# Loads of the expert stage issued one 128-row tile at a time, instead of two tiles in one DMA

## The chip, the core and the metric

The kernel runs on one NeuronCore of a Trainium2 chip. The metric is the device time of one execution in microseconds (us); lower is better. The engines are named as in the profile: PE (TensorE, matmul) with its weight loads PEld, DVE (VectorE), ACT (ScalarE), POOL (GpSimd) and SP (SyncE), which computes nothing and issues DMAs.

## What is computed

16 batches of 512 tokens with 256 features pass a layer norm, a linear attention and a feed-forward part with 16 routed experts (4 for each token) and a shared one:

```python
xn = _layernorm(x, axis=-1)
x = x + attn(xn) + ffn(xn)
# ffn, T = 8192 tokens, H = 256, E = 16 experts, I = 128
combine = _route(x, gate_weight)                 # (T, E), 4 weights of a token are not zero
up = jnp.einsum('th,ehi->eti', x, expert_up)
down = jnp.einsum('eti,eih->eth', jax.nn.silu(up), expert_down)
moe_out = jnp.einsum('te,eth->th', combine, down)
shared = jax.nn.silu(x @ shared_up) @ shared_down
```

The kernel computes an expert only for the tokens that are routed to it.

## The kernel before

**First stage** (to about 469 us of the profiled span). For each batch the kernel normalises, computes the attention, the shared expert and the routing. POOL scatters each token's row of features and weights into `by_expert`, a table in DRAM with a region for each expert. A row of it has two halves of `RW` = 272 floats: the token's features with its routing weights, and the running sum of its outputs.

**Expert stage** (the rest). The work is cut into `UNITS` = 143 units. A unit is one expert and `UR` = 256 rows of the table, held in SBUF as two tiles of 128 rows. A unit `u` passes these steps:

- SP: `load_rows(u)` brings the unit's first halves into `f_rows[u % 8]` (names `x_in` and `xn` in the trace, line 424). It waits until PE has done `up` of unit `u - 6` (semaphore `fu_done`), which frees the buffer. `load_sums(u)` brings the second halves into `f_y[u % 8]` (`xn`, line 434), after waits on `added[k]`, the landings of earlier units' scatters (line 433). The first row's number is in a register, read from a table in SBUF; `four_from` (line 323) reads the numbers of four units in one TENSOR_LOAD, for the row numbers and for each of the four classes of `added`.
- PE: `turn_rows(u)` (line 1446) waits for `rows_loaded[u % 8]` and transposes the rows into PSUM, 4 matmuls a unit; `up` (line 316, into `bank_x`) and `down` (line 316, into `bank_a` or `bank_y`) follow.
- ACT: rounds the transposed rows (698), the silu (719), rounds its result (724), stages the weights (708).
- DVE: copies the unit's weights out of the rows (1242, waits for `rows_loaded`), the low parts (1245, 1268), then `sum_up(u)` (1251 and 1257, waits for `acc_loaded[u % 8]`), which adds the outputs to the sums.
- POOL: scatters the sums back with two indirect DMAs (574).

On each engine the order is written out by hand. SP's is `load_rows(0)`, `load_rows(1)`, ..., with sums three units behind rows:

```python
            ROWS_AHEAD = 7
            SUMS_AHEAD = 4
            for u in range(UNITS + ROWS_AHEAD):
                if u < UNITS:
                    load_rows(u)
                if 0 <= u - (ROWS_AHEAD - SUMS_AHEAD) < UNITS:
                    load_sums(u - (ROWS_AHEAD - SUMS_AHEAD))
```

After the last unit SP stores the sums to the output in eight DMAs (451).

Of the kernel before, what the change touches and what calls it, by code (L numbers as in the profile page):

```python
# [12 lines left out]
P = 128  # L13
# [8 lines left out]
def attention_and_routed_ffn(  # L22
# [33 lines left out]
    YB = 8  # L56
# [23 lines left out]
    with ExitStack() as ctx:  # L80
# [3 lines left out]
        def sem(name):  # L84
            return ctx.enter_context(nc.semaphore(name))
# [4 lines left out]
        def wait(eng, s, value):  # L90
            if value > 0:
                eng.wait_ge(s, value)

        def reused(t, shape, at=0, partitions=P):
            names = " ".join("abcd"[:len(t.shape) - 1])
            flat = t[tuple(slice(None) for _ in t.shape)].rearrange(f"p {names} -> p ({names})")
            size = 1
            for n in shape:
                size *= n
            names = " ".join("abcd"[:len(shape)])  # L100
            return flat[0:partitions, at:at + size].rearrange(f"p ({names}) -> p {names}",
                                                              **dict(zip("abcd", shape)))
# [150 lines left out]
        RB = 8  # L253
        f_y = [reused(xn, (2, RW), (i + 4) % 8 * 2 * RW) for i in range(YB)]
        f_rows = [reused(xn, (2, RW), (YB + i) * 2 * RW) for i in range(4)]
# [37 lines left out]
        rows_loaded = [sem(f"rows_loaded{i}") for i in range(RB)]  # L293
        fx_done, fx_hi, fx_lo, fw_ready, w2_ready = sems("fx_done", "fx_hi", "fx_lo", "fw_ready", "w2_ready")
        fu_done, fs_done, fh_hi, fh_lo, fd_done = sems("fu_done", "fs_done", "fh_hi", "fh_lo", "fd_done")
        acc_loaded = [sem(f"acc_loaded{i}") for i in range(YB)]
# [8 lines left out]
        def scatters_until(c):  # L305
            return BATCH_SCATTERS * (c // NB + 1)

        def adds_until(u):
            return PRIMED + 32 * (u // CLS + 1)
# [11 lines left out]
        def four_from(engine, i, u, low, high):  # L321
            if u % 4 == 0:
                fours[engine, i] = fours.get((engine, i), ())[-4:] + nc.values_load_multi_w_load_instructions(
                    table[i:i + 1, u // P, u % P:u % P + 4], engines=[engine], min_val=low, max_val=high,
                    skip_runtime_bounds_check_because="the plan makes every entry, and makes it within these bounds")[1]
            return fours[engine, i][-4 + u % 4]
# [6 lines left out]
        def expert_from(words, u):  # L333
            return (words[u // PACK] >> 4 * (u % PACK)) & (E - 1)
# [16 lines left out]
        def _(sp):  # L351
# [34 lines left out]

            def unit_rows(first_row, half):
                return by_expert[bass.ds(first_row, UR), half * RW:(half + 1) * RW].rearrange(
                    "(s p) r -> p s r", p=P)

            zero_rows = [SPARE] + [FIRST + e * REGION for e in range(E)] + [OVER + i * OVER_ROWS for i in range(OVERS)]

# [22 lines left out]
            row_of = {}  # L415

            def load_rows(u):
                wait(sp, fu_done, u - RB + 3)
                row_of[u] = four_from(mybir.EngineType.SP, 0, u, 0, SLOTS - UR)
                if u < EARLY:  # L420
                    sp.wait_ge(scattered[(B - 1) % NB], four_from(mybir.EngineType.SP, 2 + CLS, u, scatters_until(B - 1 - NB),
                                                                  scatters_until(B - 1)))
                    sp.sem_inc(rows_whole, 1)
                sp.dma_start(f_rows[u % RB], unit_rows(row_of[u], 0)).then_inc(rows_loaded[u % RB], 16)

            def load_sums(u):
                if u == 4:
                    sp.wait_ge(scattered[(B - 1) % NB], scatters_until(B - 1))
                if u >= YB:
                    sp.wait_ge(added[(u - YB) % CLS], adds_until(u - YB))  # L430
                for k in range(CLS):
                    sp.wait_ge(added[k], four_from(mybir.EngineType.SP, 2 + k, u, PRIMED, PRIMED + 32 * UNITS))
                    sp.sem_inc(sums_free, 1)
                sp.dma_start(f_y[u % YB], unit_rows(row_of.pop(u), 1)).then_inc(acc_loaded[u % YB], 16)

            ROWS_AHEAD = 7
            SUMS_AHEAD = 4
# [5 lines that stand above are left out]
# [286 lines left out]
        def _(dve):  # L729
# [507 lines left out]

            def rows_low(u):
                expert = expert_from(experts, u)
                dve.wait_ge(rows_loaded[u % RB], 16 * (u // RB + 1))  # L1240
                wait(dve, y_ready, u - 3)
                V.tensor_copy(w2[:, u % 4, :], f_rows[u % RB][:, :, bass.ds(expert + D, 1)]  # L1242
                              .rearrange("p s o -> p (s o)")).then_inc(w2_ready, 1)
                dve.wait_ge(fx_hi, u + 1)
                V.tensor_tensor(f_l[u % 4], A[u % 2][:, :].rearrange("p (c s t) -> p c s t", c=KD, s=2),  # L1245
                                f_h[u % 4].bitcast(F32), ALU.subtract).then_inc(fx_lo, 1)

            def sum_up(u):
                expert = expert_from(experts, u)
                dve.wait_ge(acc_loaded[u % YB], 16 * (u // YB + 1))  # L1250
                V.tensor_tensor(f_id[:, u % YB, :], f_y[u % YB][:, :, bass.ds(expert + D, 1)].bitcast(U32)
                                .rearrange("p s o -> p (s o)"), nowhere[:, u % YB, :], ALU.max).then_inc(id_ready, 1)
                dve.wait_ge(fd_done, u + 1)
                dve.wait_ge(w2_ready, u + 1)
                for tile in range(2):
                    y = f_y[u % YB][:, tile, 0:D]
                    last = V.scalar_tensor_tensor(out=y, in0=f_dn[u % 2][tile][:, 0:D], scalar=w2[:, u % 4, tile:tile + 1],  # L1257
                                                  in1=y, op0=ALU.mult, op1=ALU.add)
                last.then_inc(y_ready, 1)

            rows_low(0)
            rows_low(1)
            for u in range(UNITS + 1):
                if u + 2 < UNITS:
                    rows_low(u + 2)
                if u < UNITS:
                    dve.wait_ge(fh_hi, u + 1)
                    V.tensor_tensor(f_hl[u % 2], f_hid[u % 2], f_hh[u % 2].bitcast(F32), ALU.subtract  # L1268
                                    ).then_inc(fh_lo, 1)
                if u >= 1:  # L1270
                    sum_up(u - 1)

        @block.tensor
        def _(pe):
# [164 lines left out]
            last.then_inc(plan_turned, 1)  # L1439

            def turn_rows(u):
                pe.wait_ge(rows_loaded[u % RB], 16 * (u // RB + 1))
                wait(pe, fx_lo, u - 1)
                for h in range(KD):
                    for tile in range(2):
                        last = T_.transpose(A[u % 2][:, (2 * h + tile) * P:(2 * h + tile + 1) * P],  # L1446
                                            f_rows[u % RB][:, tile, h * P:(h + 1) * P], ident[:, :])
                last.then_inc(fx_done, 1)

            pe.wait_ge(plan_ready, 1)  # L1450
            experts = load_experts(mybir.EngineType.PE)
            turn_rows(0)
            turn_rows(1)
            for u in range(UNITS + 1):
                if u < UNITS:
# [50 lines left out]
```

## Time and profile before

| | before |
|---|---|
| median of 3 runs | 972.61 us (971.91 to 973.69) |
| time of the profiled execution | 966.78 us |
| its span, first to last instruction | 964.8 us |
| PE, DVE, ACT, POOL busy, of the span | 80%, 73%, 57%, 60% |
| first rows loaded, last scatter issued | 469.2 us, 947.7 us |

The profiled execution is 5.8 us below the median of the runs and 2.0 us above its own span. The granted TensorE clock was 0.929 of full speed over the span. Busy shares leave out SP: its instructions wait, move registers or issue DMAs, and the profile shows when they start and how long they take.

### The profile page before, as it was taken

What the parts mean: (1) busy time and instruction counts of PE and PEld (TensorE: products, weight loads), DVE (VectorE), ACT (ScalarE), POOL (GpSimd) and SP (SyncE); (2) the same over time, 40 slices, a digit from 0 to 9 for tenths busy, and PEclk for the clock granted to TensorE, in tenths of its full rate; (3) what the DMA queues carried; (4) which work ended last, traced back from release to release, by engine and by line L of the source; (5) the groups of instructions that cost most, each with busy time, mean ns of one, the idle gap of its engine ahead of it and who ended that gap; (6) DMA issues with size and microseconds to landing.
All of it is one profiled execution on the core that took longest, in us unless ns stands there. A gap on an engine that the chain in (4) does not pass through costs nothing. (4 is left out here: it accounts for less than half of the span.)

```text
span 964.8 us, 19765 instructions
## 1 busy us (share of the span) xinstructions
PE 768.8 (80%) x5264; PEld 704.2 (73%) x5264; DVE 700.7 (73%) x2390; ACT 553.1 (57%) x1142; POOL 581.4 (60%) x581
## 2 busy tenths in 40 slices
PE   4999999999999999997377767687676776776760
PEld 4899999999899988886266666676675775765750
DVE  5989898888888999999466555665556665656550
ACT  5677677676677766663155545554545544555440
POOL 1067766666777766666556565665555566656662
PEclk9999999999999999999599899998889888999795
DMA  5245554554445433332599888888887887888889
GB/s 156 71 171 193 186 176 179 194 187 175 149 159 188 146 129 129 114 116 112 177 288 284 239 266 266 252 261 268 245 252 250 270 267 247 265 264 261 249 277 304
DMA packets 142316, 202.15 MB, mean 210 GB/s; under 512 B 16176, under 2 KB 117184, under 8 KB 142208
## 3 DMA queue, kind: packets, MB, share of 16 engines
q1 hardware_dynamic: 114144, 116.47, 41.8%
q0 software_dynamic: 28064, 84.43, 22.8%
q8 instruction: 45, 0.74, 0.3%
q14 instruction: 63, 0.52, 0.2%
HBM read 104.19 MB, written 105.04 MB: 217 GB/s over the span
## 5 line engine op out<-in xcount | busy, mean ns | idle before, releaser
L574 POOL DMA_INDIRECT rows_by_expert<-xn,f_id x286 | 279.8, 978 | 194.4 <-issue 64.5
L490 POOL DMA_INDIRECT rows_by_expert<-xn,slots_now x192 | 196.9, 1026 | 122.8 <-PE bank_a L316 59.1
L1245 DVE TENSOR_TENSOR xt_l<-bank_a,xt_h 128x512 fp32r<-128x512 f32 x143 | 98.3, 687 | 97.1 <-ACT xt_h L698 67.4
L719 ACT ACTIVATE hid<-bank_x 128x256 f32<-128x256 f32 x143 | 55.3, 387 | 147.3 <-PE bank_x L316 71.5
L698 ACT CAST xt_h<-bank_a 128x512 fp32r<-128x512 f32 x143 | 83.8, 586 | 77.7 <-PE bank_a L1446 49.7
L316 PE MATMUL bank_y<-we,hs_h 128*128 x284 | 68.0, 333 | 68.4 <-DVE hs_l L1268 45.3
L316 PE MATMUL bank_a<-we,hs_h 128*128 x288 | 70.0, 337 | 61.9 <-DVE hs_l L1268 42.5
L316 PEld LDWEIGHTS bank_y<-we,hs_h 128*128 128x128 f32 x284 | 49.4, 210 | 82.3 <-issue 82.2
L316 PEld LDWEIGHTS bank_a<-we,hs_h 128*128 128x128 f32 x288 | 51.4, 216 | 75.0 <-issue 74.6
L316 PE MATMUL bank_y<-ws,hs_h 128*128 128x256 f32 x512 | 94.4, 282 | 1.4 <-DVE hs_l L997 1.4
L316 PE MATMUL bank_x<-xt_h,ws 128*128 128x512 f32 x256 | 92.1, 401 | 0.0
L496 POOL DMA_INDIRECT rows_by_expert<-xn,slots_now x64 | 80.0, 1250 | 17.9 <-issue 14.2
L316 PEld LDWEIGHTS bank_y<-ws,hs_h 128*128 128x128 f32 x512 | 80.9, 188 | 4.4 <-DVE hs_l L997 1.6
L1257 DVE SCALAR_TENSOR_TENSOR xn<-bank_a,w,xn 128x256 f32<-128x256 f32 x144 | 62.6, 476 | 15.1 <-PE bank_y L316 10.9
L316 PE MATMUL bank_y<-ws,hs_l 128*128 128x256 f32 x256 | 72.3, 282 | 0.0
L1257 DVE SCALAR_TENSOR_TENSOR xn<-bank_y,w,xn 128x256 f32<-128x256 f32 x142 | 61.8, 476 | 13.3 <-PE bank_a L316 10.2
L316 PE MATMUL bank_x<-xt_h,k_h 128*128 128x256 f32 x288 | 70.8, 306 | 0.0
L316 PE MATMUL bank_x<-xt_h,k_l_p 128*128 128x256 f32 x284 | 68.1, 301 | 0.0
L651 ACT ACTIVATE k_f<-bank_a,minus_one 128x256 f32<-128x256 f32 x64 | 30.4, 475 | 57.5 <-issue 41.4
L1268 DVE TENSOR_TENSOR hs_l<-hid,hs_h 128x256 fp32r<-128x256 f32 x143 | 60.0, 420 | 2.8 <-ACT hs_h L724 2.8
L724 ACT CAST hs_h<-hid 128x256 fp32r<-128x256 f32 x143 | 59.5, 416 | 0.1
L1446 PE MATMUL bank_a<-ident,xn 128*128 128x128 f32 x288 | 48.6, 296 | 12.6 <-DMA xn<-rows_by_expert 12.6
(289 smaller groups left out, 2427.7 us busy)
## 6 DMA issues: line engine op xcount, KB each, us to landing
xn<-rows_by_expert SPq DMA_DIRECT2D x215, 272.0 KB
x_in<-rows_by_expert SPq DMA_DIRECT2D x71, 272.0 KB
rows_by_expert<-spare SPq DMA_DIRECT2D x22, 544.0 KB
x_in<-in_L_attn_x_dram SPq DMA_DIRECT2D x16, 512.0 KB
out_dram<-rows_by_expert SPq DMA_DIRECT2D x8, 1024.0 KB
rows_by_expert<-xn,f_id POOLq DMA_INDIRECT x286
rows_by_expert<-xn,slots_now POOLq DMA_INDIRECT x256
w_raw<-in_L_ffn_expert_up_dram SPq DMA_DIRECT2D x32, 64.0 KB
```

Of the source, the lines that this page charges most:

```text
L316: last = nc.tensor.matmul(dst, a, b, start=start and k == 0, stop=stop and k == n - 1, skip_group_check=mixed)
L490: G.indirect_dma_start(out=half_rows[:, :], in_=xn[:, c % NB, s, 0:RW], in_offset=None, out_offset=bass.IndirectOffsetOnAxis(ap=slots_now[ ...
L496: G.indirect_dma_start(out=by_expert[:, :], in_=xn[:, c % NB, s, :], in_offset=None, out_offset=bass.IndirectOffsetOnAxis(ap=slots_now[:, ...
L574: G.indirect_dma_start(out=half_rows[:, :], in_=f_y[u % YB][:, tile], in_offset=None, out_offset=bass.IndirectOffsetOnAxis(ap=f_id[:, u % ...
L651: S_.activation(k_f[:, s, :], A[s][:, 0:D], ACT.Exp, bias=minus_one[:, 0:1])
L698: S_.copy(f_h[u % 4], A[u % 2][:, :].rearrange("p (c s t) -> p c s t", c=KD, s=2)).then_inc(fx_hi, 1)
L719: S_.activation(f_hid[u % 2], X[u % 2][:, 0:UR], ACT.Silu).then_inc(fs_done, 1)
L724: S_.copy(f_hh[u % 2], f_hid[u % 2]).then_inc(fh_hi, 1)
L1245: V.tensor_tensor(f_l[u % 4], A[u % 2][:, :].rearrange("p (c s t) -> p c s t", c=KD, s=2), f_h[u % 4].bitcast(F32), ALU.subtract).then_inc ...
L1257: last = V.scalar_tensor_tensor(out=y, in0=f_dn[u % 2][tile][:, 0:D], scalar=w2[:, u % 4, tile:tile + 1], in1=y, op0=ALU.mult, op1=ALU.add)
L1268: V.tensor_tensor(f_hl[u % 2], f_hid[u % 2], f_hh[u % 2].bitcast(F32), ALU.subtract).then_inc(fh_lo, 1)
L1446: last = T_.transpose(A[u % 2][:, (2 * h + tile) * P:(2 * h + tile + 1) * P], f_rows[u % RB][:, tile, h * P:(h + 1) * P], ident[:, :])
```

## The change

`unit_rows` now yields the tiles one by one, and `load_rows` and `load_sums` issue one DMA for each tile of 128 rows. Both DMAs of a unit count on the semaphore of the buffer, so what was a wait for 16 (times the turn of the buffer) is now a wait for 32. Nobody starts on one tile alone. Bytes, buffers, and the order of units are as they were.

```diff
             def unit_rows(first_row, half):
                 return by_expert[bass.ds(first_row, UR), half * RW:(half + 1) * RW].rearrange(
-                    "(s p) r -> p s r", p=P)
+                    "(s p) r -> s p r", p=P)
...
-                sp.dma_start(f_rows[u % RB], unit_rows(row_of[u], 0)).then_inc(rows_loaded[u % RB], 16)
+                for tile in range(2):
+                    sp.dma_start(f_rows[u % RB][:, tile], unit_rows(row_of[u], 0)[tile]).then_inc(rows_loaded[u % RB], 16)
...
-                sp.dma_start(f_y[u % YB], unit_rows(row_of.pop(u), 1)).then_inc(acc_loaded[u % YB], 16)
+                first_row = row_of.pop(u)
+                for tile in range(2):
+                    sp.dma_start(f_y[u % YB][:, tile], unit_rows(first_row, 1)[tile]).then_inc(acc_loaded[u % YB], 16)
...
             def rows_low(u):
                 expert = expert_from(experts, u)
-                dve.wait_ge(rows_loaded[u % RB], 16 * (u // RB + 1))
+                dve.wait_ge(rows_loaded[u % RB], 32 * (u // RB + 1))
...
             def sum_up(u):
                 expert = expert_from(experts, u)
-                dve.wait_ge(acc_loaded[u % YB], 16 * (u // YB + 1))
+                dve.wait_ge(acc_loaded[u % YB], 32 * (u // YB + 1))
...
             def turn_rows(u):
-                pe.wait_ge(rows_loaded[u % RB], 16 * (u // RB + 1))
+                pe.wait_ge(rows_loaded[u % RB], 32 * (u // RB + 1))
```

SP's program, early in the expert stage, before. An ISA row computes the address of the DMA behind it in registers; waits are named where they stand ahead of a row:

```order
L323 TENSOR_LOAD q_f [waits fu_done]
L424 ISA
L424 DMA xn<-rows_by_expert 128x2x272
L434 ISA [waits added0,added1,added2,added3]
L434 DMA xn<-rows_by_expert 128x2x272
L424 ISA [waits fu_done]
L424 DMA xn<-rows_by_expert 128x2x272
```

The same kind of place now (lines 424 and 434 have become 425 and 437):

```order
L323 TENSOR_LOAD q_f [waits fu_done]
L425 ISA
L425 DMA x_in<-rows_by_expert 128x272
L425 ISA
L425 DMA x_in<-rows_by_expert 128x272
L437 ISA [waits added1,added0,added2,added3]
L437 DMA xn<-rows_by_expert 128x272
L437 ISA
L437 DMA xn<-rows_by_expert 128x272
L425 ISA [waits fu_done]
```

Each load has become two pairs of ISA and DMA, and no wait stands between the two. In the whole of SP's program that is 286 pairs more, two for each of 143 units; the table reads and the waits stand where they stood. The other engines have the same instructions in the same order.

## Rows read from the trace of the kernel before

**Rows 1.** Windows view, all engines, steady part of the expert stage (busy us, instructions).
```profile
core 0: us, PE busy (x) PEld busy (x) DVE busy (x) ACT busy (x) POOL busy (x), PEclk, DMA share, GB/s
500.00:920.00 420.00, 301.31 (x2056) 277.09 (x2054) 259.75 (x772) 220.06 (x517) 251.91 (x258) 0.90 0.84 259
```

**Rows 2.** Waits view, PE, 500 to 920 us: in total, times, longest.
```profile
PE bank_y L316 <- DVE hs_l L1268: 42.5, 21, 4.4
PE bank_a L316 <- DVE hs_l L1268: 37.5, 19, 4.2
...
```

**Rows 3.** Windows view of line 1446 alone (PE's transposes, 4 matmuls a unit).
```profile
core 0: us, PE busy (x) PEld busy (x), PEclk, DMA share, GB/s
480.00:500.00 20.00, 5.62 (x32) 4.05 (x31) 0.91 0.88 273
...
500.00:920.00 420.00, 85.30 (x516) 66.15 (x516) 0.90 0.84 259
```

**Rows 4.** View of line 1446: what ended PE's idle time before it (us, times).
```profile
  DMA xn<-rows_by_expert: 26.3, 6
```

**Rows 5.** Waits view, SP's queue, 500 to 920 us: all of it.
```profile
SPq L433 <- DMA rows_by_expert<-xn,f_id: 31.2, 31, 3.4
SPq L424 <- remote: 7.2, 6, 1.6
SPq L424 <- PE bank_x L316: 7.0, 8, 1.5
SPq L323 <- PE bank_x L316: 2.1, 3, 1.0
SPq L323 <- remote: 0.4, 1, 0.4
```

**Rows 6.** Timeline of SP's queue (start us, us of one issue).
```profile
484.40 0.37 SPq L424 DMA_DIRECT2D x_in<-rows_by_expert  x1
485.25 0.37 SPq L434 DMA_DIRECT2D xn<-rows_by_expert  x1
...
502.08 0.37 SPq L434 DMA_DIRECT2D xn<-rows_by_expert  x1
502.64 0.37 SPq L424 DMA_DIRECT2D x_in<-rows_by_expert  x1
...
504.62 0.70 SPq L424 DMA_DIRECT2D x_in<-rows_by_expert  x1
505.66 0.37 SPq L434 DMA_DIRECT2D xn<-rows_by_expert  x1
506.62 0.37 SPq L424 DMA_DIRECT2D x_in<-rows_by_expert  x1
```

**Rows 7.** Views of lines 424, 433, 323: ns min/median/max, first and last start.
```profile
L424 SPq FUSED_REGOPS  x131: 3/37/699, 500.3 to 919.4; - x131
L424 SPq MOVE x_in<-rows_by_expert x66: 2/29/709, 501.0 to 917.9; - x66
...
L433 SPq EVENT_SEMAPHORE  x572: 3/17/4505, 478.3 to 929.1; - x191
...
L323 SPq TENSOR_LOAD <-q_f x161: 3/298/1400, 499.6 to 913.9; - x161
```

**Rows 8.** DMA view, 500 to 920 us: queue, packets, MB, share of 16 engines.
```profile
q1 hardware_dynamic: 70515, 72.22, 61.8%
```

**Rows 9.** DMA view, 500 to 920 us: issues of the loads.
```profile
xn<-rows_by_expert SPq DMA_DIRECT2D x194, 272.0 KB
x_in<-rows_by_expert SPq DMA_DIRECT2D x66, 272.0 KB
```

## The prediction, made before the changed kernel ran

> **What bounds the kernel now.** The change touches only the expert stage, so I read that stage. First the windows view of its steady part [rows 1]: in 420 us PE is busy 301 us (72%), DVE 62%, ACT 52%, POOL 60%, and the DMA engines 84% at 259 GB/s. No engine is full. Then who is waited for: PE's longest waits end with DVE's low part of the hidden rows [rows 2], the chain PE, ACT, DVE, PE of one unit. No wait of PE in this stretch ends with a load; the waits that do, 26.3 us in 6 times [rows 4], lie at the start. So loads are early, and the pace is one unit in 3.26 us: 516 transposes, 4 a unit, are 129 units in 420 us [rows 3].
>
> Last the queue that the change makes longer, SP's. The reader should see two things in it. It waits little: its waits add up to 47.9 us [rows 5], 0.37 us a unit. And it is not idle in the rest. Two gates hold SP back: rows wait for `up` of an older unit, sums for landings of old scatters. A queue with time to spare would stand at one of them in every unit. The waits view names 49 such stops [rows 5], for the 260 loads [rows 9]. So in most units SP stands at no gate and runs as fast as it can, in 3.26 - 0.37 = 2.89 us a unit.
>
> **What the change adds on SP.** Each load gets a second pair of address computation and DMA. The nearest row is exact: where SP goes from a sums load to the next rows load with no stop, the two DMAs start 0.56 us apart (502.08 to 502.64) [rows 6], and between them stand just the first DMA's issue (0.37 us), one register operation and one move (medians 37 and 29 ns [rows 7]), the rest being gaps. The added pair is this sequence, so 0.56 us, and 1.12 us a unit with two loads.
>
> **What SP's unit costs.** From rows to sums without a stop, four semaphore instructions included, it is 0.85 us (484.40 to 485.25) [rows 6]; back to rows 0.56. That is 1.41. Table reads: 161 for 129 units, median 298 ns [rows 7], 0.37 us a unit. Together 1.78 us, if nothing disturbs it. The difference to the 2.89 us above, 1.11 us, is time that the waits view doesn't name: the same rows show it as steps of 1.04 and 0.96 us where 0.85 and 0.56 would do (from 504.62 on) [rows 6], and as maxima of 699 ns and more for instructions of 30 ns [rows 7]. It is either a slowness of SP under load, which stays, or waits that the view missed, which an SP that is later would not have to make.
>
> - If all of it is missed waits: 1.78 + 1.12 = 2.90 us a unit, under 3.26. SP fits.
> - If all of it stays: 2.89 + 1.12 = 4.01 us. SP sets the pace, 0.75 us a unit slower.
>
> I take two thirds of the 1.11 us as staying (0.74), nearer to the upper end, because the delays also fall on the register instructions, which wait for nothing: 1.78 + 0.74 + 1.12 = 3.64 us a unit. SP then becomes the bound; PE, DVE, ACT and POOL, which have room at 3.26, wait for loads. (3.64 - 3.26) x 143 units = 54 us.
>
> **The start of the stage.** From 480 to 500 us PE turns 8 units in 20 us, 2.5 us each [rows 3], and this is where it already waits for loads. Counting all 143 units at 3.26 leaves out that these 8 went faster: at the new pace they lose 8 x (3.26 - 2.5) = 6 us more.
>
> **What costs nothing.** Bytes stay. Each new DMA ends with its counts on 16 engines: taking them as whole packets, 32 more a unit, 2 on each engine. A packet of the hardware queue takes 0.618 x 16 x 420 us / 70,515 = 59 ns [rows 8], so at most 0.12 us a unit, of 0.52 us that the engines are free (16% of 3.26); below this they cost nothing. The second tile's data starts 0.56 us later than now; consumers wait for both tiles, but no PE wait ends with a load in the steady part [rows 2], so as long as SP keeps its lead this is hidden, and if the lead is gone it is in SP's sum already. Nothing else is queued on SP but the waits on `added` and the table reads, and they stand behind the longer issue; who waits for them is again the loads. The drain after the last unit, POOL's last scatters and the stores, is as before. The wait for 32 instead of 16 is free.
>
> **Whether an issue is small.** A unit's load is 272 KB [rows 9], 278.5 thousand bytes, 1.08 us at 259 GB/s; a half is 0.54 us, so an added pair of 0.56 us is as long as the transfer it starts. The Trainium skill, page DMA: Bandwidth & Descriptors, section Issuing engines are not separate DMA queues, says that the sequencer's time to start a DMA is usually small relative to the DMA itself. By that rule the added time would be 0 and the kernel the same. For a half load the trace disagrees.
>
> **The sum.** 54 + 6 = 60 us on the profiled execution's 966.8 us: 1026.8. The median of the runs is 5.8 us above it, so 1033 us.
>
> **Rivals.**
>
> - *SP just fits.* All of the 1.11 us are missed waits; 2.90 us a unit is under 3.26. For it: the delays come in lumps, and may be of the record rather than of the queue. Against it: SP's few stops. The steady pace stays, but in the start SP's 2.90 meets PE's 2.5: 8 x 0.4 = 3 us; 976 us, slower by 0.35%. Chance 0.15.
> - *No change.* The same, and the loads in the start are hidden too, since SP's own waits there for scatters cover the added issues: 973 us. This is also what the skill's rule gives. Chance 0.10.
> - *Everything stays.* 4.01 us a unit: 0.75 x 143 + 6 = 113 us, 1086 us. It is the upper end of the forecast's own term. If the new instructions are slowed as the old ones are, by 2.89 / 1.78, the 1.12 becomes 1.82 us, 4.71 us a unit, and the time 966.8 + 1.45 x 143 + 6 + 5.8 = 1186 us. Chance 0.05 for beyond 1088.
> - *Faster.* One mechanism: a DMA of one tile reads 128 rows in the order in which they lie, and half as much stands in a queue at once, so POOL's scatters get their turn on the 16 engines sooner. SP's 31.2 us of waits on their landings [rows 5] would shrink; at most all go, 942 us. It decides only if SP has more than 1.12 us a unit to spare and if landings set the pace, and PE's waits [rows 2] name none. Chance 0.05.
> - *Forecast*: SP sets the pace, between 3.3 and 4.0 us a unit. Chance 0.65.
>
> **How the numbers follow.** The time is the forecast's, 1033. What a measurement can tell from no change is about 0.2%, 2 us. The range goes from the rival that just fits, 976, to the end where everything stays, 1088; it leaves out no change, faster, and the multiplied cost, 0.20 together. Slower is forecast, just fits and multiplied, 0.85; same 0.10; faster 0.05.
>
> **What the changed profile would show.** Right: two issues of a load 0.5 to 0.6 us apart; SP's named waits near zero, since it never reaches a gate; waits of PE's transposes or DVE's weight copy on DMA landings all through the stage, not in the start alone; a unit in about 3.6 us; DMA share down from 0.84 to about 0.75; PE's busy time nearly the same, with perhaps a lower granted clock as it idles more. Wrong: SP's named waits still a few tenths of a microsecond a unit and no wait of PE on a load, which would say that SP had time to spare. The weakest step is the split of the 1.11 us.

## The result, and the profile after

The changed kernel takes 1039.64 us (median of 4 runs, 1035.4 to 1041.53), the kernel before on the same chip 973.15 us (4 runs, 971.91 to 975.35). The ratio is 1.0675, 95% interval 1.0636 to 1.0713: slower. The profiled execution took 1041.53 us, with a span of 1039.4 us, 74.6 us more than before, at a granted clock of 0.912. Lines have moved: rows are loaded at 425, sums at 437, the wait for older scatters is 434, PE's transposes are 1449, DVE's weight copy 1245.

Read in the order in which the prediction read the kernel before. First the windows of the steady part, all engines:

```profile
core 0: us, PE busy (x) PEld busy (x) DVE busy (x) ACT busy (x) POOL busy (x), PEclk, DMA share, GB/s
520.00:980.00 460.00, 303.81 (x1993) 276.53 (x1992) 260.76 (x746) 218.13 (x498) 238.40 (x248) 0.88 0.76 227
```

and of the transposes alone (columns as in [rows 3]):

```profile
480.00:500.00 20.00, 5.36 (x26) 3.85 (x27) 0.79 0.65 189
520.00:980.00 460.00, 92.53 (x496) 60.94 (x496) 0.88 0.76 227
```

496 transposes are 124 units in 460 us, **3.71 us a unit**, where [rows 3] gave 3.26 and the prediction 3.64. Every engine is less busy than in [rows 1] (PE 66% of the stretch, was 72%), and so are the DMA engines, 0.76 at 227 GB/s after 0.84 at 259. So none of these became the bound. The 8 fast units at the start are gone too: 26 transposes are 6.5 units in the same 20 us, 3.1 us each, where there were 8 at 2.5.

Who is waited for has turned round. Waits view of SP's queue, 520 to 980 us, all of it:

```profile
SPq L323 <- DMA rows_by_expert<-xn,f_id: 3.4, 12, 0.4
SPq L434 <- DMA rows_by_expert<-xn,f_id: 1.6, 3, 0.7
```

Waits view of PE, the same stretch, its longest rows:

```profile
PE bank_a L1449 <- DMA x_in<-rows_by_expert: 70.4, 44, 3.6
PE bank_a L1449 <- DMA xn<-rows_by_expert: 69.1, 43, 3.6
```

and of DVE:

```profile
DVE w L1245 <- DMA x_in<-rows_by_expert: 19.8, 22, 2.8
DVE w L1245 <- DMA xn<-rows_by_expert: 16.4, 17, 1.7
```

SP stands at a gate for 5.0 us in all, against 47.9 us before [rows 5], though the stretch is longer. PE waited on no load in the steady part before; now it waits 139.5 us on loads, 87 times in 124 units. In [rows 2] the low part of the hidden rows was what PE waited for; it is no longer among the long ones. SP's queue, its issues from 700 us on (start, time of the row, number of issues in it):

```profile
699.97 0.85 SPq L425 DMA_DIRECT2D x_in<-rows_by_expert  x2
701.39 0.87 SPq L437 DMA_DIRECT2D xn<-rows_by_expert  x2
702.44 0.85 SPq L425 DMA_DIRECT2D x_in<-rows_by_expert  x2
705.86 0.85 SPq L437 DMA_DIRECT2D xn<-rows_by_expert  x2
```

and the instructions of the rows' line (ns min/median/max):

```profile
L425 SPq FUSED_REGOPS  x248: 2/37/1398, 521.5 to 979.2; - x124
L425 SPq DMA_DIRECT2D x_in<-rows_by_expert x125: 3/333/1397, 519.8 to 969.6; - x125
L425 SPq MOVE x_in<-rows_by_expert x124: 4/29/719, 521.6 to 969.5; - x124
L425 SPq MOVE xn<-rows_by_expert x124: 2/29/726, 530.3 to 979.3; - x124
```

Two issues take 0.85 us together and one 0.333 us, so they start 0.52 us apart. An issue of 128 rows takes 333 ns, of 2 x 128 rows 0.37 us [rows 6]. Where nothing is in the way, rows to sums is 1.42 us (699.97 to 701.39) and back 1.05 (701.39 to 702.44); before, 0.85 and 0.56. Then 3.42 us pass between rows and sums (702.44 to 705.86), with no wait named. The trace has in them four table reads of 0.30 us each, which stand there in every fourth unit, and a step of 0.72 us just ahead of the first issue; that issue, of 333 ns elsewhere, is recorded with 22 ns. The page has the chain of work that ended last, and the loads' DMA queue:

```profile
SPq 16%; issue 15%; DMA 11%; PE 6%; POOL 2%; DVE 2%; ACT 1%; POOLq 0%; another core or an unknown queue 0%; DVEq 0%; ACTq 0%
...
q1 hardware_dynamic: 118720, 116.49, 40.0%
```

SP's share of the chain was 0% before and is the largest now. The queue has 4,576 packets more (118,720 after 114,144), 16 for each of the 286 added DMAs, and the same bytes.

**Where the 74.6 us lie.** 143 units at 3.71 instead of 3.26 are 64 us; the start, by the prediction's own count, 6 us; and in this execution the first rows load came at 474.4 us instead of 469.2, 5 us. Of these 5 us, 3 arise before any changed instruction: the weight loads ahead of it began at 466.6 us instead of 463.5. In the repeat of the same kernel (below) the first rows load came at 470.7 us.

### The profile page after: what moved, and what is told of

It reads as the page before. It is cut to its first block, busy times and chain, and to the rows that moved or that the text cites. A ratio compares the mean times of both kernels' runs of the same rounds, so it can differ in the third digit from the quotient of the medians.

```text
span 1039.4 us, 20623 instructions
## 1 busy us (share of the span) xinstructions
PE 784.7 (75%) x5264; PEld 715.4 (69%) x5264; DVE 712.5 (69%) x2390; ACT 559.8 (54%) x1142; POOL 575.2 (55%) x581
## 3 DMA queue, kind: packets, MB, share of 16 engines
q1 hardware_dynamic: 118720, 116.49, 40.0%
## 4 chain that ended last, share of the span: by engine, by line
SPq 16%; issue 15%; DMA 11%; PE 6%; POOL 2%; DVE 2%; ACT 1%; POOLq 0%; another core or an unknown queue 0%; DVEq 0%; ACTq 0%
SPq L425 6%; SPq L437 5%; DMA rows_by_expert<-xn,f_id 5%; DMA x_in<-rows_by_expert 4%; SPq L323 3%; POOL rows_by_expert L577 2%; PE bank_a L1449 2%; DMA xn<-rows_by_expert 2%; SPq L434 2%; PE bank_a L316 1%; PE bank_x L316 1%; PE bank_y L316 1%; ACT xt_h L701 1%; DVE xt_l L1248 1%; DVE hs_l L1271 1%
## 5 line engine op out<-in xcount | busy, mean ns | idle before, releaser
L577 POOL DMA_INDIRECT rows_by_expert<-xn,f_id x286 | 275.0, 962 | 264.8 <-DVE f_id L1254 79.9
L1449 PE MATMUL bank_a<-ident,xn 128*128 128x128 f32 x288 | 55.2, 323 | 101.4 <-DMA xn<-rows_by_expert 92.3
L1449 PE MATMUL bank_a<-ident,x_in 128*128 128x128 f32 x284 | 52.4, 314 | 84.2 <-DMA x_in<-rows_by_expert 80.0
L1449 PEld LDWEIGHTS bank_a<-ident,xn 128*128 128x128 f32 x288 | 36.1, 159 | 115.1 <-DMA xn<-rows_by_expert 105.0
L1449 PEld LDWEIGHTS bank_a<-ident,x_in 128*128 128x128 f32 x284 | 34.8, 157 | 96.8 <-DMA x_in<-rows_by_expert 91.7
L316 PE MATMUL bank_x<-xt_h,k_h 128*128 128x256 f32 x288 | 72.9, 313 | 0.0
L316 PE MATMUL bank_x<-xt_h,k_l_p 128*128 128x256 f32 x284 | 70.9, 310 | 0.0
```

The lines of the kernel that those rows point to most:

```text
L316: last = nc.tensor.matmul(dst, a, b, start=start and k == 0, stop=stop and k == n - 1, skip_group_check=mixed)
L577: G.indirect_dma_start(out=half_rows[:, :], in_=f_y[u % YB][:, tile], in_offset=None, out_offset=bass.IndirectOffsetOnAxis(ap=f_id[:, u % ...
```

## The experiments

The theory, A: SP's queue has become the bound, by the time that its added instructions take. Rivals: B, the loss is in the transfers (half loads, more packets, another order on the 16 engines); C, SP had no time to spare at all, so every added piece costs its full length (0.52 us a unit, 74 us, for one added pair). Ratios are to the kernel before on the same chip.

| run | us | ratio (95%) | us a unit |
|---|---|---|---|
| e1 rows split | 987.22 | 1.0192 (1.0162 to 1.0222) | 3.36 |
| e2 sums split | 985.08 | 1.0184 (1.0137 to 1.0232) | 3.34 |
| e3 delay only | 1087.64 | 1.1237 (1.1209 to 1.1265) | 4.05 |
| e4 four DMAs a load | 1403.11 | 1.4490 (1.4453 to 1.4528) | 6.28 |
| e5 changed, half rows | 925.75 | 1.0816 (1.0792 to 1.0841) | 3.03 |
| e6 before, half rows | 854.41 | 0.9994 (0.9977 to 1.0010) | 2.51 |
| e7 changed, reads of 8 | 917.85 | 1.0712 (1.0685 to 1.0738) | 2.94 |
| e8 before, reads of 8 | 856.23 | 1.0000 (0.9985 to 1.0014) | 2.54 |
| e9 changed again | 1035.26 | 1.0632 (1.0599 to 1.0665) | 3.70 |
| e10 second tile from ACT | 1002.19 | 1.0313 (1.0277 to 1.0348) | 3.44 |
| e11 added reads | 973.21 | 0.9999 (0.9972 to 1.0026) | 3.31 |
| e12 sums one unit later | 974.87 | 1.0005 (0.9987 to 1.0022) | 3.33 |

The kernel before had 967.59 us beside e1 to e4 (7 runs), **856.37 us** beside e5 to e8 (19 runs) and 974.05 us beside e9 to e12 (23 runs). These are three chips; the second is 12% faster with the same program. Us a unit are from the windows view (520 to 920 us; 480 to 780 on the second chip), PE's instructions over 16 a unit. The kernel before has 3.27 by the same count (1960 in 400 us).

### One half of the change: e1 and e2

e1, against the changed kernel (DVE's wait at the sums is for 16 again):

```diff
-                first_row = row_of.pop(u)
-                for tile in range(2):
-                    sp.dma_start(f_y[u % YB][:, tile], unit_rows(first_row, 1)[tile]).then_inc(acc_loaded[u % YB], 16)
+                sp.dma_start(f_y[u % YB], unit_rows(row_of.pop(u), 1).rearrange("s p r -> p s r")).then_inc(acc_loaded[u % YB], 16)
```

> Only the loads of rows are split; the sums' loads are one DMA as before. Theory A (SP's time for its instructions sets the pace of the changed kernel, 3.71 us a unit): one added pair instead of two takes about 0.56 us off, 3.15 us, which is under the 3.26 us of the kernel before, so that nearly all of the loss is gone in the steady part, and only the start loses: 975 to 985 us. Theory B (the split transfers themselves are slower, by their smaller size or more completions): each split load costs the same, half of the loss: about 1006 us.

e2, against the changed kernel (PE's and DVE's waits on rows are for 16 again):

```diff
-                for tile in range(2):
-                    sp.dma_start(f_rows[u % RB][:, tile], unit_rows(row_of[u], 0)[tile]).then_inc(rows_loaded[u % RB], 16)
+                sp.dma_start(f_rows[u % RB], unit_rows(row_of[u], 0).rearrange("s p r -> p s r")).then_inc(rows_loaded[u % RB], 16)
```

> Only the loads of sums are split. Theory A: as with rows alone, one added pair, 975 to 985 us. Theory B: half of the loss, about 1006 us. If rows and sums differ by more than 5 us, it matters what is behind the pair in the queue.

Measured: +19.6 and +17.5 us over the kernel before on this chip. The times expected were for the chip of the result: A asked for 2 to 12 us over the kernel before, B for 33. Both runs lie between, nearer to A. Waits view of SP's queue in e1, 520 to 920 us, all of it:

```profile
SPq L434 <- DMA rows_by_expert<-xn,f_id: 3.9, 6, 0.7
SPq L323 <- DMA rows_by_expert<-xn,f_id: 2.7, 7, 0.7
```

and of PE, its longest rows:

```profile
PE bank_a L1447 <- DMA xn<-rows_by_expert: 36.1, 25, 3.6
PE bank_a L1447 <- DMA x_in<-rows_by_expert: 35.6, 22, 2.6
PE bank_a L316 <- DVE hs_l L1269: 17.2, 12, 3.5
```

The halves cost 37 us together, the whole change 66. With C each half would cost 74 us; a loss that grows faster than its cause belongs to a queue that first uses up the time it has to spare. The border is not sharp: one added pair brings 0.52 us to SP's unit and 0.09 us to the pace, and has already used up SP's waits (6.6 us left) and made PE wait 71.7 us for loads. Rows and sums are alike, though PE and DVE's weight copy wait for rows, and only the last step of a unit for sums; what both share is SP.

### SP's time without any change to the transfers: e3 and e4

e3, against the kernel before, behind the rows' issue, and the same behind the sums':

```diff
                 sp.dma_start(f_rows[u % RB], unit_rows(row_of[u], 0)).then_inc(rows_loaded[u % RB], 16)
+                for _ in range(8):
+                    sp.sem_inc(spent, 1)
```

> The kernel before, every load in one DMA; behind each of the two issues of a unit SP makes 8 more semaphore increments that nobody waits for, 8 x 0.07 = 0.56 us, as long as the added pair. Theory A: it is SP's time alone, so as slow as the changed kernel, 1030 to 1045 us. Theory B: 973 us, since no transfer is changed.

Timeline of SP's queue in e3:

```profile
699.66 0.37 SPq L425 DMA_DIRECT2D xn<-rows_by_expert  x1
700.97 0.37 SPq L437 DMA_DIRECT2D xn<-rows_by_expert  x1
```

The windows of its steady part, all engines:

```profile
520.00:920.00 400.00, 260.21 (x1581) 241.24 (x1580) 206.92 (x589) 173.65 (x395) 188.34 (x196) 0.80 0.72 207
```

PE's longest waits there:

```profile
PE bank_a L1451 <- DMA xn<-rows_by_expert: 58.6, 29, 5.5
PE bank_a L1451 <- DMA x_in<-rows_by_expert: 55.3, 29, 5.4
```

Rows to sums is 1.31 us with nothing in the way, 0.46 us above the 0.85 of [rows 6]: 0.058 us for each increment, 0.92 us a unit. Not one DMA differs from the kernel before, and yet PE now waits 113.9 us for loads and a unit takes 4.05 us. So B is not needed: time on SP's queue alone makes a loss of this kind, and a larger one. The size was missed: A expected 57 to 72 us over the kernel before, and e3 has 120. 0.92 us of bare time (the time of the instructions without any delay) cost 0.79 us of pace (4.05 after 3.26), the change's 1.04 us only 0.45. What differs is the number of added instructions, 16 here and 6 there, and their kind; which of the two it is, no run separated (e11 was meant to).

e4 splits each load once more, against the changed kernel (rows shown, sums alike, waits for 64):

```diff
-                    sp.dma_start(f_rows[u % RB][:, tile], unit_rows(row_of[u], 0)[tile]).then_inc(rows_loaded[u % RB], 16)
+                    for h in range(2):
+                        at = slice(h * 64, (h + 1) * 64)
+                        sp.dma_start(f_rows[u % RB][at, tile], unit_rows(row_of[u], 0)[tile, at]).then_inc(rows_loaded[u % RB], 16)
```

> Each load in four DMAs of 64 rows, so four pairs a unit more than in the changed kernel. Theory A: 4 x 0.52 to 0.56 = 2.1 to 2.2 us a unit more, 5.8 us a unit, 300 to 315 us more than the changed kernel, 1340 to 1355 us. Theory B has no price for a pair; if the delays that SP shows beside its bare instructions come with each instruction, up to 1.6 times that, 1530 us.

Windows of e4's steady part, all engines:

```profile
520.00:920.00 400.00, 213.16 (x1019) 196.28 (x1018) 138.31 (x383) 114.59 (x256) 123.15 (x128) 0.64 0.50 134
```

Its timeline of SP's queue (the first row is sums, the second rows):

```profile
699.72 2.43 SPq L441 DMA_DIRECT2D xn<-rows_by_expert  x4
702.34 2.42 SPq L427 DMA_DIRECT2D x_in<-rows_by_expert  x4
```

The rows' line, ns min/median/max:

```profile
L427 SPq DMA_DIRECT2D xn<-rows_by_expert x128: 279/468/1524, 519.7 to 917.7; - x128
```

Four issues in 2.43 us are 0.65 us apart, 8 a unit 5.2 us; with the table reads (0.37) and the four waits (0.28) these are some 5.9 us, and the unit takes 6.28. SP's queue has no named wait at all. A's forecast, 5.8 us and 1340 to 1355 us, took 0.52 to 0.56 us for each of the added pairs and all of the delays as before; with 0.65 us for all eight pairs the bare time is 0.9 us longer than by that count, and the delays are smaller (6.28 - 5.9 = 0.4 us instead of 0.9). The DMA engines are half idle: the same bytes, at 134 GB/s. A 64-row issue costs 468 ns, more than one of 2 x 128 rows. TensorE's granted clock is 0.64 in this stretch, a mean of its two levels of 1.2 and 2.4 GHz; PE was idle 47% of it.

### Fewer bytes, and fewer table reads: e5 to e8

e5 and e6 leave out the first 128 of the 256 features in every load of rows (old data stands in their place), in the changed kernel and in the kernel before. e5's edit:

```diff
-                    sp.dma_start(f_rows[u % RB][:, tile], unit_rows(row_of[u], 0)[tile]).then_inc(rows_loaded[u % RB], 16)
+                    sp.dma_start(f_rows[u % RB][:, tile, P:], unit_rows(row_of[u], 0)[tile, :, P:]).then_inc(rows_loaded[u % RB], 16)
```

> The changed kernel, but the loads of rows bring 144 of the 272 columns of each row, so the first 128 features of the experts' input are left from earlier data; the instructions are the same. A unit moves 705 instead of 836 thousand bytes. Before e1 to e4 I took SP's time beside its bare instructions as a constant; the runs show it as about 0.05 us for each instruction of a unit at a DMA share of 0.72 to 0.76, and 0.01 at a share of 0.50. If it comes from the DMA traffic, the unit falls from 3.71 to 3.4 or 3.5 us, 995 to 1010 us. If it is SP's own, the time stays, 1035 to 1042 us.

> The kernel before with the same cut, 144 of 272 columns in the loads of rows (first 128 features left from earlier data). If the traffic of the DMA engines also sets the pace of the kernel before, 16 percent fewer bytes give up to 0.4 us a unit, 915 to 950 us; if it is the chain of PE, ACT and DVE alone, 965 us or within 3 us of the kernel before.

e7 and e8 read the planner's table for 8 units at once instead of 4, in the changed kernel and in the kernel before:

```diff
-            if u % 4 == 0:
-                fours[engine, i] = fours.get((engine, i), ())[-4:] + nc.values_load_multi_w_load_instructions(
-                    table[i:i + 1, u // P, u % P:u % P + 4], engines=[engine], min_val=low, max_val=high,
+            if u % 8 == 0:
+                fours[engine, i] = fours.get((engine, i), ())[-8:] + nc.values_load_multi_w_load_instructions(
+                    table[i:i + 1, u // P, u % P:u % P + 8], engines=[engine], min_val=low, max_val=high,
...
-            return fours[engine, i][-4 + u % 4]
+            return fours[engine, i][-8 + u % 8]
```

> The changed kernel, but SP reads its tables for eight units at once, five reads in eight units instead of ten. If SP's time sets the pace: 0.62 reads a unit less at 0.34 us and 0.05 us, 0.24 us a unit, 34 us, so 1000 to 1010 us. If the split transfers set it: 1040 us.

> The kernel before with the same cut of table reads. If SP has time to spare there: no change, within 3 us. If SP already holds the kernel back now and then (its unit near the pace), 3 to 15 us faster.

Windows of e5, all engines:

```profile
480.00:780.00 300.00, 224.52 (x1585) 203.92 (x1584) 203.75 (x598) 178.00 (x398) 191.45 (x199) 0.94 0.79 235
```

and of e6:

```profile
480.00:780.00 300.00, 257.82 (x1913) 230.24 (x1912) 238.20 (x719) 214.09 (x478) 228.37 (x235) 0.99 0.91 279
```

Fewer bytes change nothing in the kernel before (0.9994), and with them the changed kernel still loses 8%; e7, which moves all bytes on the same chip, is 8 us faster than e5. So bytes set the pace of neither. The number of DMAs and packets is not changed by this, so of B only the bytes fall here. The reads tell less. The 8-entry read is longer, as e7's row of line 323 has it:

```profile
L323 SPq TENSOR_LOAD <-q_f x64: 520/548/887, 485.8 to 770.9; - x64
```

64 of these in 102 units are 0.34 us a unit; 1.25 reads of 299 ns were 0.37. In e8 the median is 643 ns. The edit took nearly nothing off SP, so it can't tell how much a shorter SP gives back, and the time expected of e7 was not put to the test. e8 is the kernel before, unchanged in time.

What this chip adds is a second look at SP's delays. e5's rows line:

```profile
L425 SPq FUSED_REGOPS  x198: 37/46/56, 480.2 to 779.6; - x198
L425 SPq DMA_DIRECT2D xn<-rows_by_expert x100: 332/333/1073, 479.8 to 773.3; - x100
L425 SPq MOVE xn<-rows_by_expert x99: 29/29/37, 480.2 to 773.3; - x99
```

No register instruction lasts longer than 56 ns here, where the chip of the result has maxima of 1398 ns for the same one. A unit takes 3.03 us, 0.21 above the bare 2.82 (worked out below). The kernel before runs at 2.54 us here, so SP's bare time alone is above the pace, and the loss is larger in ratio than on the slower chip: 1.07 to 1.08 in e5 and e7. The unmodified changed kernel was not run on this chip. Another difference is that PE already waits for loads in the kernel before here: 32.9 us in the 300 us of e8, with SP 70.6 us at the scatters' gate.

### A repeat, and ways to give the time back: e9 to e12

e9 is the changed kernel once more, beside the others of its chip.

> The changed kernel itself, beside the three others on one chip, since chips differ: e1 to e4 had 967.6 us for the kernel before, e5 to e8 856.4 us. Where the kernel before takes some 970 us: 1.065 to 1.07 of it. Where it takes some 856 us: SP's unit is 2.8 us of bare instructions against a pace of 2.54 us, and 3.0 us were seen in e5, so 1.08, 920 to 930 us. If the loss needs the delays of the first kind of chip: 1.03 or less.

1.0632, just under the 1.065 to 1.07 expected, and 3.70 us a unit.

e10 lets ACT issue the second tile of each rows load from unit 8 on; SP keeps the first tile and both of the sums. In ACT's loop, against the changed kernel (its waits for the first stage's scatters left out here):

```diff
-                for tile in range(2):
+                for tile in range(2 if u < 8 else 1):
...
+                if 2 <= u < UNITS - 6:
+                    v = u + 6
+                    first_row = four_from(mybir.EngineType.Activation, 0, v, 0, SLOTS - UR)
+                    act.dma_start(f_rows[v % RB][:, 1], by_expert[bass.ds(first_row, UR), 0:RW].rearrange(
+                        "(s p) r -> s p r", p=P)[1]).then_inc(rows_loaded[v % RB], 16)
```

> As the changed kernel, every load in two DMAs, but from unit 8 on the second tile of the rows is issued by ACT. SP keeps one added pair, ACT gets about 0.6 us a unit. Theory A (SP's time): as with rows or sums alone, 1.00 to 1.02 of the kernel before. Theory B (the split itself): as the changed kernel, 1.065 to 1.08.

The issues that ACT makes in e10, 135 for units 8 to 142:

```profile
xn<-rows_by_expert ACTq DMA_DIRECT2D x68, 136.0 KB
x_in<-rows_by_expert ACTq DMA_DIRECT2D x67, 136.0 KB
```

PE's waits on loads, 520 to 920 us:

```profile
PE bank_a L1459 <- DMA x_in<-rows_by_expert: 41.8, 29, 3.8
PE bank_a L1459 <- DMA xn<-rows_by_expert: 34.5, 29, 3.2
```

All transfers are those of the changed kernel; a quarter of the issues stands on another queue, and 33 of the 61 us that e9 lost on this chip come back. PE's waits on loads fall to 76.3 us, from 105.6 in e9 in the same stretch. B asked for no gain here, since all transfers stay split and only the issuer of some is another. A gain is what A says; the size is not: 1.0313 lies above A's 1.00 to 1.02, and above e1's 1.0192 (on another chip), in which SP has the same load. ACT now spends the issue and an address itself, and e10 has one more split load than e1; whether the rest, about 12 us, is ACT's time or the split itself was not separated.

e11 was to give the kernel before three more table reads a unit.

> The kernel before, and behind each load of rows SP reads the table three more times for nothing, 3 x 0.34 = 1.02 us a unit in 3 instructions, where the changed kernel adds 1.04 us in 6 and e3 added 0.94 us in 16. If the delays come with each instruction (0.05 us each on the slower kind of chip), it lies below the changed kernel, 1.035 to 1.05 of the kernel before; if only SP's time counts, it is as the changed kernel. On the faster kind of chip, where SP shows no such delays, as the changed kernel, 1.07 to 1.08.

It tests nothing: no instruction used the reads, and the built program has none of them (154 reads in 400 us, 1.25 a unit, as before). It is a second copy of the kernel before, and shows how close two copies come: 0.9999 (0.9972 to 1.0026).

e12 issues the sums one unit later, in the kernel before, so that SP doesn't stand at their gate:

```diff
-            SUMS_AHEAD = 4
+            SUMS_AHEAD = 3
```

> The kernel before with SUMS_AHEAD = 3 for 4, so that SP comes to each load of sums one unit later and stands less often behind landings of scatters, with rows queued behind it. On the faster kind of chip, where SP waited 70 us in 300 there and PE 33 us for rows: 3 to 12 us faster. On the slower kind, where PE waits for no load in the steady part: same, within 2 us. If the sums then come too late, slower by 3 us or more, with waits of DVE on them.

Waits view of SP in e12, 520 to 920 us:

```profile
SPq L323 <- PE bank_x L316: 24.9, 17, 2.9
SPq L424 <- PE bank_x L316: 17.5, 15, 2.6
...
SPq L433 <- DMA rows_by_expert<-xn,f_id: 4.9, 9, 1.4
```

The 31.2 us at the scatters' gate [rows 5] are 4.9, and SP stands as much longer at the rows' gate. The time is the same, 1.0005. So SP's waits before were spare time on this kind of chip, and landings of scatters set nothing. On the second chip, where SP waits longest for them, e12 was not run. No experiment beat the kernel before.

## Why the prediction was right

The forecast was 1033 us, between 976 and 1088, slower with 0.85; measured 1039.64. The likeliest case was the one that came, SP's queue as the new bound.

- **What bounds the kernel** (loads early, PE's chain sets the pace, SP nearly full without looking it): right for SP. e12 moves SP's waits and leaves the time alone; e1 and e2 show that half of the change is enough to spend them. That PE's chain sets the pace is read from PE's waits [rows 2]; no run shortened that chain.
- **The added pair, 0.56 us, 1.12 a unit**: 0.52 and 1.04. The sequence was the right one, but its DMA was one of 2 x 128 rows, 0.37 us; one of 128 rows takes 333 ns.
- **SP's bare unit, 1.78**: with the pairs it is now 1.42 + 1.05 + 0.37 for the table reads = 2.84 by the timeline, 1.78 + 1.04 = 2.82 by the sum. Right.
- **Two thirds of the 1.11 us stay, 0.74**: the weakest step, a guess between two ends, and its size came out near by luck as much as by reading. The measured rest is 3.71 - 2.82 = 0.89 us, 0.85 without SP's named waits. How it divides is not shown: it can be four fifths of the old 1.11, or less of that and some delay on the new instructions, which the forecast's term had at zero. A fit by the number of instructions comes out for two runs. By the code, SP has 11.25 a unit before (3 for a load, 4 waits, 1.25 reads), 17.25 now and 27.25 in e3; 0.89 / 17.25 is 0.052 us an instruction, and for e3 4.05 - 1.78 - 0.92 = 1.35 over 27.25 is 0.050. But the same fit fails in e4, with 29.25 instructions and 0.013 us each, and leaves 0.3 of 1.0 us open in e1. The number of delays doesn't grow with it either: counted in the traces, a start of an SP instruction comes more than 0.4 us later than the median for that place 1.9 times a unit in the kernel before (its named waits included), 1.5 times in the changed kernel, 2.25 in e3 and 0.4 in e4. So the fit is no rule.
- **The pace, 3.64, (3.64 - 3.26) x 143 = 54 us**: 3.71, 64 us. This is the term that was short.
- **The start, 6 us**: 6.5 units instead of 8 in the 20 us of the start, and 6 (24 transposes) in e9, whose first load came at 470.7 us, near the 469.2 of the kernel before. The 1.5 to 2 units are 6 to 7 us at 3.7.
- **Packets and bytes cost nothing**: for the bytes e6 shows it. For the packets it is not shown alone: 4,576 more in the whole run are the 32 a unit of the bound, and the loads' queue now has 71,494 packets and 56.1% of the 16 engines' time from 520 to 980 us, which with [rows 8] is 2.08 us a unit after 2.01, inside the bound of 0.12. e3 needs no added packet for its loss; the 12 us between e1 and e10 leave room for a small cost.
- **An issue is small beside its DMA**: the Trainium skill, DMA: Bandwidth & Descriptors, section Issuing engines are not separate DMA queues, says "usually small relative to the DMA itself"; taken as a rule it would have given no change. Here a pair takes 0.52 us and the half load, by an estimate from the 259 GB/s of [rows 1], 0.54 us; in e4 a pair takes 0.65 us and its quarter load, by the same estimate, 0.27 us. The measurement decides: for loads of this size the issue is not small.
- **Signs in the profile**: issues 0.52 us apart, SP's waits near zero, PE and DVE waiting on loads all through, DMA share 0.76, a clock of 0.88 after 0.90: each as named. PE's busy time for a unit rose a little, 303.81 / 124 = 2.45 us after 301.31 / 129 = 2.34, at the lower clock; it had the room.
- **The rivals**: "just fits" and "no change" fell with SP's 5.0 us of waits. "Faster" fell by its own condition: it wanted landings to set the pace, and e12 shows that they don't on a chip of this kind. "Everything stays" was 4.01 us a unit, 0.30 above the measured 3.71. Its sum gives 1086 us, 2 us under the 1088 that the range has for the same end.

**Open**: what the delays are. They come in steps of about 0.7 us (maxima of 719 and 726 ns for moves of 29). They don't follow the DMA traffic alone: e4 has few at a DMA share of 0.50, but the second chip has few as well (0.21 us a unit in e5, at a share of 0.79), and its register instructions stay short in e7 at 0.91. What differs between the chips no run told, nor was it tried why two of them differ by 12% in the whole kernel.

Part of a delay may be work and not loss. These issues of the kernel before, of 0.37 us elsewhere, are recorded with almost no length:

```profile
700.39 0.02 SPq L434 DMA_DIRECT2D xn<-rows_by_expert  x1
...
706.93 0.01 SPq L434 DMA_DIRECT2D xn<-rows_by_expert  x1
```

Of the changed kernel's 496 issues from 520 to 980 us, 110 are recorded with under 0.1 us, and 107 of these stand within five SP instructions behind a step of more than 0.4 us; on the second chip there is none. So some of an issue's own time seems to lie in the step recorded ahead of it, and the steps can't be added up as time lost; only the whole unit less the bare time can. Whether the recording itself has a part in the steps was not tried.

## What to carry to other kernels

Before splitting a transfer, add up what its queue issues in one period: instructions times their spacing, and compare with the period. A queue with few named waits, though it has gates, may be nearly full, even if it is on no critical chain and its engine counts as idle. An added issue first uses up what is left, and then it costs more: here the first added pair of 0.52 us cost 0.09 us a unit, and the two together 0.45. Nothing comes back for it where the consumer waits for both halves anyway. The bare time alone can be too short an estimate: in e3, 0.92 us of it made the unit 0.79 us longer, more than the 1.04 us of the change did.

## What the runs showed of the hardware

- The same program (the kernel before) takes 856 us on one chip and 968 to 974 on others.
- Of the changed kernel's loss on one chip, 61 us, 33 came back when ACT issued a quarter of SP's DMAs (e10 against e9), with the transfers the same.
- An issue costs by its shape and not by its bytes: 373 ns for 2 x 128 rows, 333 for 128, 468 for 64 (with half the bytes it is still 333 in e5 and 373 in e6).
- SP's register read of 4 entries takes 298 ns, of 8 entries 548 in e7 and 643 in e8 (medians): batching them saved next to nothing. A semaphore increment takes 0.058 us of the queue (e3).
- SP's register instructions of 29 to 37 ns last up to 0.7 us and more on some chips (e1, e3, e9 and the chip of the result), and on another never over 56 ns in e5 and 42 ns in e7, at DMA shares of 0.79 and 0.91. The cause is open.
